# A selective-scan block with routing: two more of 32 slots get u from GpSimd, its statistics become powers and products, and x times D is made by ScalarE

## The chip, the cores and the metric

One core of one Trainium2 chip runs the whole kernel. The metric is device time in microseconds (us), the median over runs; the profile is of one further execution. The engines are named as in the profile: PE is TensorE, DVE VectorE, ACT ScalarE, POOL GpSimd, SP SyncE, which issues the transfers.

## The reference, cut to what matters

```python
x = resid + layernorm(mamba(layernorm(resid)))     # (2, 2048, 512)
out = x + layernorm(moe_bias(layernorm(x)))
# mamba: E = 1024 channels, N = 16 states
rn = r * rsqrt(mean(r * r) + eps) * norm_w
skip, x_in = rn @ W_skip, rn @ W_in
x = silu(conv4(x_in) + conv_b)
delta = softplus(x @ W_delta_1 @ W_delta_2 + b_delta_2)
B, C = x @ W_B, x @ W_C
h = h * exp(delta * A) + (delta * x) * B            # scan over time
y = sum_n(h * C) + x * W_D
mamba = r + (y * silu(skip)) @ W_out
# moe_bias: softmax over 64 experts, the 8 largest weights w
out = h2 * sum(w) + sum_k(w_k * expert_bias[k])
```

All is float32. A layernorm of rows needs their mean and variance, and x is normed twice in a row (layernorm, then the mean of squares).

## The kernel before, in words

The 2 x 2048 rows are cut into 16 chunks of T = 256. Six jobs work on a chunk one after another: norm, prep (projection, convolution, delta, B, C), scan, gate, mix (skip projection, y times silu(skip), W_out) and route (the second half of the reference). The loop is a pipeline of steps: in step i, chunk i + 3 is in norm, i + 2 in prep, i in scan, i - 1 in gate, i - 2 in mix and i - 3 in route. Each step has 32 slots. In each slot one scan unit is done: one of the 16 states for 256 of the channels over SPAN = 512 time steps, so a pair of chunks is scanned together. The order of work on each engine is written out by hand: every engine walks the same steps and slots, and side jobs stand at fixed slot numbers, `s`, counted from the job's own step (-4 is slot 28 of the step before, 41 is slot 9 of the step after).

A scan unit takes this way. ACT makes the decay exp(delta A) (`decay`, L728), and u = (delta x) B is made in one of two ways. In a **plain** slot POOL multiplies `dx_q` by `b_all`, a row of B that DMA has spread over all partitions, into `operand` (`make_u`, L597), and the decay goes to `bank` in PSUM. In a **turned** slot ACT scales the transposed `dx_t` by B (`make_ut`, L747, four instructions a slot), and PE transposes it back into `bank` (`turn_u`, L1152, eight a slot); the decay then goes to `operand`. `PLAIN_SLOTS` says which slots are plain. `bank` has no second buffer: whoever writes it, PE or ACT, waits for the scan before. `operand`, `h` and `hc` have three. DVE runs the scan itself (L971, two of 512 steps a slot), one slot's state over. POOL multiplies h by C (`weigh`, L613), one slot behind DVE, and PE transposes that onto `y_sum`, summing over the states (`add_y`, L1157), two slots behind. At the first of 16 states `add_y` also brings in x times D (L1175): a matmul of `x_q`, loaded from DRAM where `x` was stored, by `diag_d`, a diagonal matrix of D.

In its slot ACT first does the side jobs, then half of u two slots on, the first decay one slot on, the other half, the second decay. PE first transposes u for the next slot and adds y of two slots before, in turns, then does side work: the projections and transposes of the other jobs. DVE does its scan first, POOL first `weigh`, then `make_u` for two slots on.

Prep works on pairs of channel tiles, p = 0 to 3, at slots `TAPPED` = -5, 1, 6, 10: there ACT makes the convolution's first tap (`hv`, L709) and DVE the others (L1034); four slots on ACT makes the tanh (L816) and DVE `x` (L1017).

The statistics of four row blocks (xn, z, x1 and o; `mvx`, `mvz`, `mvh`, `mvo`) are started by DVE (`moments`, L946 and L949, mean and variance) and finished by POOL (`rstd` and `minus_mean_times`, L571 to L579), which adds eps, raises to the power -0.5 and multiplies by the negated mean, two values a partition. ACT then scales the rows with them (L709). After a small instruction whose result the next one needs, `link` makes the engine wait for it.

## Time and profile before

| | us |
|---|---|
| median of 3 runs | 2184.05 (2183.57 to 2187.59) |
| the profiled execution, its own time | 2178.91 |
| its span | 2177.1 |
| busy: PE matmul | 1893.4 (87%) |
| busy: POOL | 1859.3 (85%) |
| busy: DVE | 1726.6 (79%) |
| busy: ACT | 1716.2 (79%) |

The shares are over the whole span, which has a start of about 110 us before the first scan and an end of about 160 us after the last one, in which single chains of work run. The chain of work that ended last gives PE 31%, POOL 16%, DVE 15% and ACT 10% of the span.

### The profile page before, as it was taken

The page shows a single profiled execution, that of the slowest core. Times are in us where ns is not written, and L with a number is a line of the kernel's source. Part 1 is how long each engine was busy: PE and PEld are TensorE (multiplying, and loading weights), DVE is VectorE, ACT ScalarE, POOL GpSimd, SP SyncE. Part 2 cuts the span into 40 slices and gives each one's busy share as a digit, 9 for nine tenths or more (in the row PEclk, how much of TensorE's full clock was granted, in tenths as well). Part 3 has the DMA queues.
Part 4 walks back from the last instruction along what each step waited for, and adds up shares of the span by engine and source line. Part 5 has one row for each costly group of instructions (what it writes and reads, how often), then busy time and mean ns, then how long its engine had stood idle before and what let it go on. Part 6 is the DMA issues. An engine that isn't in the chain of part 4 may idle for free.

```text
span 2177.1 us, 35466 instructions
## 1 busy us (share of the span) xinstructions
PE 1893.4 (87%) x12005; PEld 1585.3 (73%) x12005; DVE 1726.6 (79%) x2529; ACT 1716.2 (79%) x3404; POOL 1859.3 (85%) x1256
## 2 busy tenths in 40 slices
PE   5677777999999998999999898999989898989883
PEld 4566767878787786878778786978778686767551
DVE  3487878898898989888888988888898978888332
ACT  3489797979888897979889897988889798888221
POOL 1299999899999999999999999999989899999312
PEclk9999898999999999999999999999999999999995
DMA  5656566765766575765756585765757464645310
GB/s 174 209 189 212 184 212 206 241 215 190 242 201 223 170 265 175 245 220 184 253 177 228 186 269 177 226 227 183 250 162 250 149 229 166 218 151 184 116 49 20
DMA packets 234672, 425.92 MB, mean 196 GB/s; under 512 B 18623, under 2 KB 134907, under 8 KB 234491
## 3 DMA queue, kind: packets, MB, share of 16 engines
q1 hardware_dynamic: 234490, 423.65, 59.0%
q8 instruction: 96, 1.57, 0.3%
q14 instruction: 86, 0.70, 0.1%
HBM read 339.18 MB, written 84.41 MB: 195 GB/s over the span
## 4 chain that ended last, share of the span: by engine, by line
PE 31%; POOL 16%; DVE 15%; ACT 10%; issue 7%; DMA 7%; DVEq 0%; SPq 0%; POOLq 0%; ACTq 0%
DVE h L971 10%; POOL hc L613 9%; PE mixed L1363 6%; PE bank L1152 6%; PE y_sum L1157 6%; PE pair_bank L1283 4%; DMA c_all<-bc_dram 4%; ACT u_t L747 3%; PE routed L1337 3%; POOL operand L597 2%; DVE hv L1034 2%; ACT operand L728 2%; DMA dx_q<-dx_dram 2%; PE routed L1237 1%; DMA dx_dram<-dx 1%
## 5 line engine op out<-in xcount | busy, mean ns | idle before, releaser
L613 POOL TENSOR_TENSOR hc<-h,c_all 128x1024 f32<-128x1024 f32 x512 | 1205.0, 2367 | 83.0 <-DVE h L971 76.0
L971 DVE TENSOR_TENSOR_SCAN h<-operand,carry,bank 128x512 f32<-128x512 f32 x528 | 649.2, 1266 | 126.1 <-PE bank L1152 112.7
L747 ACT ACTIVATE u_t<-dx_t,lbc 128x256 f32<-128x256 f32 x1408 | 631.8, 498 | 19.0 <-PE bank L1152 18.9
L1157 PE MATMUL y_sum<-ident,hc 128*128 128x128 f32 x4096 | 601.6, 278 | 7.5 <-POOL hc L613 6.8
L1152 PE MATMUL bank<-ident,u_t 128*128 128x128 f32 x2816 | 448.6, 284 | 165.5 <-DVE h L971 162.6
L1152 PEld LDWEIGHTS bank<-ident,u_t 128*128 128x128 f32 x2816 | 336.3, 145 | 274.1 <-issue 176.3
L1157 PEld LDWEIGHTS y_sum<-ident,hc 128*128 128x128 f32 x4096 | 490.7, 144 | 47.1 <-issue 27.5
L728 ACT ACTIVATE operand<-delta_q,neg_a 128x512 f32<-128x512 f32 x704 | 480.0, 711 | 0.0
L597 POOL TENSOR_TENSOR operand<-dx_q,b_all 128x1024 f32<-128x1024 f32 x160 | 378.4, 2365 | 8.4 <-DMA b_all<-bc_dram 8.4
L728 ACT ACTIVATE bank<-delta_q,neg_a 128x512 f32<-128x512 f32 x320 | 218.1, 682 | 204.1 <-DVE h L971 203.7
L971 DVE TENSOR_TENSOR_SCAN h<-bank,carry,operand 128x512 f32<-128x512 f32 x240 | 295.8, 1268 | 27.4 <-POOL operand L597 17.0
L1363 PE MATMUL mixed<-wout,ys 128*128 128x512 f32 x512 | 260.1, 602 | 3.5 <-DVE ys L1071 3.5
L1283 PE MATMUL pair_bank<-rnt,win 128*128 128x256 f32 x1024 | 247.5, 388 | 10.3 <-DVE x L1017 6.7
L1337 PE MATMUL routed<-rnt_gate,wskip 128*128 128x256 f32 x1024 | 245.3, 384 | 11.4 <-DVE thg L1059 11.4
L971 DVE TENSOR_TENSOR_SCAN h<-operand,bank 128x512 f32<-128x512 f32 x176 | 206.9, 1208 | 47.6 <-PE bank L1152 37.9
L1283 PEld LDWEIGHTS pair_bank<-rnt,win 128*128 128x128 f32 x1024 | 192.2, 195 | 46.2 <-issue 19.8
L1337 PEld LDWEIGHTS routed<-rnt_gate,wskip 128*128 128x128 f32 x1024 | 189.9, 193 | 36.9 <-issue 11.5
L1034 DVE SCALAR_TENSOR_TENSOR hv<-pair_bank,taps,hv 128x253 f32<-128x253 f32 (+2 forms) x384 | 184.3, 480 | 11.4
L1363 PEld LDWEIGHTS mixed<-wout,ys 128*128 128x128 f32 x512 | 81.2, 191 | 45.6 <-issue 40.9
L971 DVE TENSOR_TENSOR_SCAN h<-bank,operand 128x512 f32<-128x512 f32 x80 | 94.2, 1210 | 13.1 <-ACT bank L728 8.4
L1294 PE MATMUL pair_bank<-wlbc,x 128*128 128x160 f32 x512 | 85.7, 314 | 6.2 <-DVE x L1017 6.2
L667 POOL TENSOR_TENSOR dx<-delta,x 128x1024 f32<-128x1024 f32 x32 | 75.6, 2365 | 12.1 <-ACT delta L838 12.1
(119 smaller groups left out, 1858.5 us busy)
## 6 DMA issues: line engine op xcount, KB each, us to landing
c_all<-bc_dram SPq DMA_DIRECT2D x256, 512.0 KB, 4.3
b_all<-bc_dram SPq DMA_DIRECT2D x160, 256.0 KB, 5.5
win<-in_L_attn_W_in SPq DMA_DIRECT2D x64, 512.0 KB, 6.0
wskip<-in_L_attn_W_skip SPq DMA_DIRECT2D x64, 512.0 KB, 6.5
...
```

What stands on the lines that cost most here:

```text
L597: nc.gpsimd.tensor_tensor(operand[:, number % 3], dx_q[:, k], b_all[:, j % 2:j % 2 + 1].to_broadcast([P, 2, SPAN]), ALU.mult).then_inc(u_r ...
L613: nc.gpsimd.tensor_tensor(hc[:, number % 3], h[:, number % 3], c_all[:, j % 2, s % 2:s % 2 + 1].to_broadcast([P, 2, SPAN]), ALU.mult).then ...
L728: nc.scalar.activation(to, delta_q[:, k, q], ACT.Exp, scale=neg_a[:, et, n:n + 1]).then_inc(exp_ready.sem, 1)
L747: last = nc.scalar.activation(u_t[:, j % 2, b], dx_t[:, k, b], ACT.Copy, scale=lbc[:, stage % 2, b, DELTA + n:DELTA + n + 1])
L971: nc.vector.tensor_tensor_scan(h[:, number % 3, q], first, second, start, ALU.mult, ALU.add).then_inc(scan_done.sem, 1)
L1034: return nc.vector.scalar_tensor_tensor(out=to, in0=of, scalar=taps[:, et, k:k + 1], in1=onto, op0=ALU.mult, op1=ALU.add)
L1152: last = transpose(bank[:, q, b * P:(b + 1) * P], u_t[:, j % 2, b, q * P:(q + 1) * P], ident[:])
L1157: return matmul(to, lhsT=of, rhs=ident[:], is_transpose=True, start=start, stop=stop, skip_group_check=True)
L1283: last = matmul(pair_bank(p)[:, e * T:(e + 1) * T], win[:, p % 2, k, e * P:(e + 1) * P], rnt[:, k, :], start=(k == 0), stop=(k == KD - 1))
L1294: last = matmul(pair_banks[0][:, b * LBC:(b + 1) * LBC], x[:, et, b * P:(b + 1) * P], wlbc[:, et, :], start=(et == 0 and b == 0), stop=(et ...
L1337: last = matmul(routed[:, e * T:(e + 1) * T], wskip[:, p % 2, k, e * P:(e + 1) * P], rnt_gate[:, k, :], start=(k == 0), stop=(k == KD - 1))
L1363: last = matmul(mixed[:], ys[:, et, b * P:(b + 1) * P], wout[:, et, :], start=(et == 0), stop=(et == ET - 1))
```

## The change

It has four parts. Two more slots are plain, and the set is laid out anew: 6, 8 and 15 come in, 7 goes out. The product of x with D is made by ACT after `x` (new buffer `xd`, two of 128x256 for each pair, at slots `TAPPED` + 5 = 0, 6, 11, 15), stored in place of x, and PE brings it into `y_sum` by a transpose; `diag_d` is gone. DVE now delivers variance plus eps and the negated mean (two small reductions for each statistics, eps lies in a third column of `mv`), so that POOL is left with a power and a product; for xn both variances are raised to the power at once, four values. For o, whose rows are not divided by the softmax's sum, eps times that sum squared is made beforehand (slot 37), and half of DVE's reading of o is done a slot earlier. POOL's statistics of z move from slot 15 to 14, its addition of o from 45 to 47.

```diff
-PLAIN_SLOTS = (0, 2, 4, 7, 10, 13, 18, 22, 25, 29)
+PLAIN_SLOTS = (0, 2, 4, 6, 8, 10, 13, 15, 18, 22, 25, 29)
...
-                                        if v := due(sp, x_ready, t, p + 1):
-                                            sp.wait_ge(x_ready.sem, v)
+                                        if v := due(sp, xd_ready, t, p + 1):
+                                            sp.wait_ge(xd_ready.sem, v)
...
-                                        sp.dma_start(x_dram[side, :, 2 * p:2 * p + 2, part], x[:, 2 * p:2 * p + 2]).then_inc(
+                                        sp.dma_start(x_dram[side, :, 2 * p:2 * p + 2, part], xd[:, p % 2]).then_inc(
...
-                def rstd(to, at, var):
-
-                    link(nc.gpsimd.tensor_scalar(at, var, EPS, None, ALU.add))
-                    return nc.gpsimd.tensor_tensor(to, at, mhalf[:], ALU.pow)
-
-                def minus_mean_times(to, mv, r):
-                    link(nc.gpsimd.tensor_scalar(to, mv[:, :, 0], -1.0, None, ALU.mult))
-                    return times(to, to, r)
+                def rsqrt(to, of, halves):
+                    return nc.gpsimd.tensor_tensor(to, of, halves, ALU.pow)
...
-                                    link(rstd(now[:, 2], small["varx"][:], mvx[:, :, 1]))
-                                    link(times(small["ms"][:], mvx[:, :, 1], now[:, 2]))
-                                if s == -3:
-                                    link(times(small["ms"][:], small["ms"][:], now[:, 2]))
-                                    link(rstd(small["r2"][:], small["ms"][:], small["ms"][:]))
-                                if s == -1:
-                                    link(times(now[:, 0], now[:, 2], small["r2"][:]))
-                                    minus_mean_times(now[:, 3], mvx, now[:, 2])
-                                    minus_mean_times(now[:, 1], mvx, now[:, 0]).then_inc(s_ready.sem, 1)
...
+                                link(nc.gpsimd.tensor_scalar(small["varx"][:], mvx[:, :, 1], 1 + EPS, EPS * EPS, ALU.mult,
+                                                             ALU.add))
+                                link(rsqrt(now[:, 0:2], both_varx, mhalf[:]))
+                                times(now[:, 2:4], small["mx"][:].unsqueeze(1).to_broadcast([P, 2, TB]),
+                                      now[:, 0:2]).then_inc(s_ready.sem, 1)
...
-                                if s == 15:
+                                if s == 14:
...
-                                    link(rstd(small["rz"][:], small["varz"][:], mvz[:, :, 1]))
-                                    minus_mean_times(small["nz"][:], mvz, small["rz"][:]).then_inc(nz_ready.sem, 1)
+                                    link(rsqrt(small["rz"][:], small["varz"][:], mhalf[:, 0]))
+                                    times(small["nz"][:], small["nz"][:], small["rz"][:]).then_inc(nz_ready.sem, 1)
...
+                                if s == 37:
...
+                                    link(times(small["eo"][:], small["se"][:], small["se"][:]))
+                                    nc.gpsimd.tensor_scalar(mvo[:, :, 2], small["eo"][:], EPS, None,
+                                                            ALU.mult).then_inc(eo_ready.sem, 1)
...
-                                    link(times(var, mvo[:, :, 1], rs))
-                                    link(times(var, var, rs))
-                                    link(rstd(ro, var, var))
-                                    link(times(ro, ro, rs))
-                                    minus_mean_times(small["no"][:], mvo, ro).then_inc(no_ready.sem, 1)
-                                if s == 45:
+                                    link(rsqrt(small["ro"][:], small["varo"][:], mhalf[:, 0]))
+                                    times(small["no"][:], small["no"][:], small["ro"][:]).then_inc(no_ready.sem, 1)
+                                if s == 47:
...
+                                for p in range(PAIRS):
+                                    if s == TAPPED[p] + 5:
+                                        if v := due(act, x_ready, t, p + 1):
+                                            act.wait_ge(x_ready.sem, v)
+                                        if v := due(act, x_stored[p % 2], t, p // 2):
+                                            act.wait_ge(x_stored[p % 2].sem, v)
+                                        for et in (2 * p, 2 * p + 1):
+                                            last = nc.scalar.activation(xd[:, p % 2, et % 2], x[:, et], ACT.Copy,
+                                                                        scale=dskip[:, et:et + 1])
+                                        last.then_inc(xd_ready.sem, 1)
...
+                def and_eps(var, minus_mean, mv, ready):
+
                     for b in range(TB):
-                        last = nc.vector.bn_stats(stat6[:, b], of[:, b])
+                        last = nc.vector.bn_aggr(mv[:, b, 0:2], stat6[:, b])
                     link(last)
...
+                    nc.vector.tensor_reduce(minus_mean, mv[:, :, 0:1], axis=AX.X, op=ALU.add, negate=True)
+                    nc.vector.tensor_reduce(var, mv[:, :, 1:3], axis=AX.X, op=ALU.add).then_inc(ready.sem, 1)
...
-                                last = matmul(y_sum[:, b, q * P:(q + 1) * P], lhsT=x_q[:, q, b * P:(b + 1) * P],
-                                              rhs=diag_d[:, 2 * quarter + q], start=b % 2 == 0 and q == 0,
-                                              stop=False, skip_group_check=True)
+                                last = add_turned(y_sum[:, b, q * P:(q + 1) * P], x_q[:, q, b * P:(b + 1) * P],
+                                                  b % 2 == 0 and q == 0, False)
```

What this moves on POOL in the slots 2 to 10 of a steady step, from the u of slot 4 on; `operand<-dx_q,b_all` is a u, `hc<-h,c_all` a `weigh`. Before:

```order
L597 TENSOR_TENSOR operand<-dx_q,b_all 128x1024
L613 TENSOR_TENSOR hc<-h,c_all 128x1024 x3
L597 TENSOR_TENSOR operand<-dx_q,b_all 128x1024
L613 TENSOR_TENSOR hc<-h,c_all 128x1024 x3
L597 TENSOR_TENSOR operand<-dx_q,b_all 128x1024
L613 TENSOR_TENSOR hc<-h,c_all 128x1024 x2
```

And after the change:

```order
L593 TENSOR_TENSOR operand<-dx_q,b_all 128x1024
L609 TENSOR_TENSOR hc<-h,c_all 128x1024 x2
L593 TENSOR_TENSOR operand<-dx_q,b_all 128x1024
L609 TENSOR_TENSOR hc<-h,c_all 128x1024
L573 TENSOR_TENSOR stats<-stats 128x2
L687 TENSOR_SCALAR mvo<-stats 128x2
L609 TENSOR_TENSOR hc<-h,c_all 128x1024
L593 TENSOR_TENSOR operand<-dx_q,b_all 128x1024
L609 TENSOR_TENSOR hc<-h,c_all 128x1024 x2
L593 TENSOR_TENSOR operand<-dx_q,b_all 128x1024
L609 TENSOR_TENSOR hc<-h,c_all 128x1024 x2
L576 TENSOR_TENSOR stats<-stats,mhalf 128x2
```

The u of slot 7 has become those of 6 and 8, the two small rows between are the part of o's statistics that needs only the softmax's sum, and of the seven rows on o that stood behind the last pair of `hc` two are left, of which the first is shown.

A little further on in POOL's row, slots 11 to 16, from the u of slot 13 on. Before:

```order
L597 TENSOR_TENSOR operand<-dx_q,b_all 128x1024
L613 TENSOR_TENSOR hc<-h,c_all 128x1024 x2
L704 TENSOR_TENSOR o<-x1,o 128x1024
L613 TENSOR_TENSOR hc<-h,c_all 128x1024 x2
L575 TENSOR_SCALAR stats<-mvz 128x2
L576 TENSOR_TENSOR stats<-stats,mhalf 128x2
L579 TENSOR_SCALAR stats<-mvz 128x2
L571 TENSOR_TENSOR stats<-stats 128x2
L613 TENSOR_TENSOR hc<-h,c_all 128x1024
```

And after:

```order
L593 TENSOR_TENSOR operand<-dx_q,b_all 128x1024
L609 TENSOR_TENSOR hc<-h,c_all 128x1024 x2
L593 TENSOR_TENSOR operand<-dx_q,b_all 128x1024
L609 TENSOR_TENSOR hc<-h,c_all 128x1024
L576 TENSOR_TENSOR stats<-stats,mhalf 128x2
L573 TENSOR_TENSOR stats<-stats 128x2
L609 TENSOR_TENSOR hc<-h,c_all 128x1024
L699 TENSOR_TENSOR o<-x1,o 128x1024
L609 TENSOR_TENSOR hc<-h,c_all 128x1024
```

A u for slot 15 has come in, z's statistics stand a slot earlier with two rows in place of four, and the addition of o stands behind them.

On ACT, slots 4 to 7 of a steady step: `u_t<-dx_t` is half of a turned u, `bank<-delta_q` and `operand<-delta_q` are decays of a plain and of a turned slot. Before, from u of slot 6 on:

```order
L747 ACTIVATE u_t<-dx_t,lbc 128x256 x2
L728 ACTIVATE operand<-delta_q,neg_a 128x512
L747 ACTIVATE u_t<-dx_t,lbc 128x256 x2
L728 ACTIVATE operand<-delta_q,neg_a 128x512
L921 ACTIVATE low<-routed 64x256
L816 ACTIVATE pair_bank1<-hv 128x512
L728 ACTIVATE operand<-delta_q,neg_a 128x512 x2
L709 ACTIVATE xn<-xn,kept 128x512 x2
L709 ACTIVATE hv<-pair_bank0,cbias,taps 128x253 x2
L747 ACTIVATE u_t<-dx_t,lbc 128x256 x2
L728 ACTIVATE bank<-delta_q,neg_a 128x512
L747 ACTIVATE u_t<-dx_t,lbc 128x256 x2
```

And after:

```order
L723 ACTIVATE operand<-delta_q,neg_a 128x512 x2
L923 ACTIVATE low<-routed 64x256
L808 ACTIVATE pair_bank1<-hv 128x512
L742 ACTIVATE u_t<-dx_t,lbc 128x256 x2
L723 ACTIVATE bank<-delta_q,neg_a 128x512
L742 ACTIVATE u_t<-dx_t,lbc 128x256 x2
L723 ACTIVATE bank<-delta_q,neg_a 128x512
L704 ACTIVATE xn<-xn,kept 128x512 x2
L818 ACTIVATE xd<-x,dskip 128x256 x2
L704 ACTIVATE hv<-pair_bank0,cbias,taps 128x253 x2
L723 ACTIVATE operand<-delta_q,neg_a 128x512 x2
L742 ACTIVATE u_t<-dx_t,lbc 128x256 x2
```

The u of slots 6 and 8 is gone from here and that of slot 7 has come in; the decays of slot 6 go to `bank` and those of slot 7 to `operand`; the product with D stands between the scaling of xn and the first tap.

## Rows read from the trace of the kernel before

**Rows 1.** Stretches: us, busy us of PE, PEld, DVE, ACT, POOL (instructions), PEclk, DMA, GB/s

```profile
895.00:900.00 5.00, 5.00 (x32) 4.57 (x31) 4.74 (x9) 4.97 (x10) 5.00 (x4) 1.00 1.02 393
...
980.00:985.00 5.00, 3.37 (x28) 2.83 (x27) 4.96 (x10) 5.00 (x12) 4.39 (x9) 1.00 0.24 76
...
864.00:987.00 123.00, 113.76 (x750) 95.85 (x750) 108.90 (x160) 107.47 (x215) 116.78 (x79) 1.00 0.66 217
...
1848.00:1971.00 123.00, 108.82 (x715) 90.46 (x716) 104.39 (x131) 100.95 (x204) 121.08 (x69) 0.96 0.53 178
```

**Rows 2.** Waits from 500 to 1900 us: total us, times, longest us

```profile
ACT bank L728 <- DVE h L971: 148.0, 89, 5.2
...
DVE h L971 <- PE bank L1152: 109.5, 121, 2.7
...
POOL hc L613 <- DVE h L971: 55.7, 49, 2.3
```

**Rows 3.** Timeline of DVE, two scans: start us, us, what [idle before <- releaser]

```profile
964.83 2.45 DVE L971 TENSOR_TENSOR_SCAN h<-operand,carry,bank 128x512 f32<-128x512 f32 x2 [1.20 <-PE bank L1152]
...
977.58 2.45 DVE L971 TENSOR_TENSOR_SCAN h<-operand,carry,bank 128x512 f32<-128x512 f32 x2 [0.75 <-PE bank L1152]
```

**Rows 4.** Timeline of POOL, the statistics of z: start us, us, what

```profile
879.69 0.22 POOL L575 TENSOR_SCALAR stats<-mvz 128x2 f32<-128x2 f32 x1
...
1002.77 0.22 POOL L575 TENSOR_SCALAR stats<-mvz 128x2 f32<-128x2 f32 x1
1003.07 0.71 POOL L576 TENSOR_TENSOR stats<-stats,mhalf 128x2 f32<-128x2 f32 x1
1003.87 0.22 POOL L579 TENSOR_SCALAR stats<-mvz 128x2 f32<-128x2 f32 x1
1004.17 0.19 POOL L571 TENSOR_TENSOR stats<-stats 128x2 f32<-128x2 f32 x1
1004.32 2.36 POOL L613 TENSOR_TENSOR hc<-h,c_all 128x1024 f32<-128x1024 f32 x1
```

**Rows 5.** Groups of instructions: count | busy us, mean ns | idle before

```profile
L747 ACT ACTIVATE u_t<-dx_t,lbc 128x256 f32<-128x256 f32 x1408 | 631.8, 498 | 19.0 <-PE bank L1152 18.9
...
L1175 PE MATMUL y_sum<-diag_d,x_q 128*128 128x128 f32 x512 | 71.5, 285 | 0.0
...
L1017 DVE SCALAR_TENSOR_TENSOR x<-pair_bank,hv 128x512 f32<-128x512 f32 x64 | 43.4, 678 | 12.4 <-ACT pair_bank L816 12.4
...
L1115 DVE TENSOR_REDUCE stats<-top 128x2 f32<-128x16 f32 x16 | 2.5, 158 | 0.0
```

**Rows 6.** Timeline of PE weight loads: start us, us, what

```profile
892.96 0.97 PEld L1175 LDWEIGHTS y_sum<-diag_d,x_q 128*128 128x128 f32 x8
893.85 0.47 PEld L1157 LDWEIGHTS y_sum<-ident,hc 128*128 128x128 f32 x4
894.29 0.47 PEld L1353 LDWEIGHTS mixed<-ident,acc 128*128 128x128 f32 x4
```

**Rows 7.** Timeline of ACT before the first scan: start us, us, what

```profile
17.73 1.52 ACT L709 ACTIVATE xn<-xn,kept 128x512 f32<-128x512 f32 x2 [3.26 <-POOL kept L571]
...
34.27 0.60 ACT L816 ACTIVATE pair_bank<-hv 128x512 f32<-128x512 f32 x1 [3.59 <-DVE hv L1034]
...
34.80 1.00 ACT L709 ACTIVATE hv<-pair_bank,cbias,taps 128x253 f32<-128x253 f32 x2
```

**Rows 8.** Waits from 1750 to 2010 us: total us, times, longest us

```profile
DVE h L971 <- POOL operand L597: 14.7, 11, 2.4
```

**Rows 9.** The chain that ended last, final stretch: start us, us, what

```profile
2133.35 1.53 ACT o L709 x2
...
2134.95 2.34 POOL o L704
...
2139.71 0.81 ACT z L709
...
2165.29 1.30 DVE stat L946 x2
```

90 lines of the change are left out of this document (47 added, 43 removed).

## The prediction

> **What bounds the kernel now.** I read the busy shares by stretch first. A whole chunk in the steady part, 864 to 987 us, has no single full engine: GpSimd is busy 116.8 of 123 us, PE 113.8, VectorE 108.9, ScalarE 107.5 [rows 1]. One chunk takes 1002.77 - 879.69 = 123.1 us, from one statistics step of z to the next [rows 4]. Cut into 5 us pieces, the same chunk falls into two parts. In the first, call it A (slots 15 to about 3, some 75 us), PE and GpSimd show 5.00 of 5.00, ScalarE 4.97 and VectorE 4.74, in the piece from 895 [rows 1]. In the second, B (slots 4 to 14, some 45 us), VectorE is full at 4.96, PE has dropped to 3.37, in the piece from 980 [rows 1].
>
> Then the waits. From 500 to 1900 us, 11.4 chunks, VectorE's scans wait 109.5 us for PE's transposes of u, 9.6 us a chunk; ScalarE waits 148.0 us for scans before it may write the next decay into the single bank, 13.0 a chunk; GpSimd waits 55.7 us for scans, 4.9 a chunk [rows 2]. No wait of a scan for GpSimd's hc stands among the long ones. So GpSimd is nearly full but lags without holding anyone; in A the pace is set by PE's and ScalarE's queues, in B by VectorE, held up where PE's side work is ahead of the transposes: 1.20 us before the scan of slot 6, 0.75 us before that of slot 9 [rows 3]. GpSimd's 4.9 us are its only slack. Late in the program this changes: from 1848 to 1971 GpSimd is busy 121.08 of 123 us [rows 1], and scans wait 14.7 us for its u [rows 8]. There it is the bound.
>
> **The change part by part, per chunk.**
>
> GpSimd. Two more multiplies of 128x1024 at 2.36 us [rows 4]; back to back the next starts about 0.04 earlier: +4.64. The statistics of z go from four instructions to two. From start to start a scalar step takes 0.30, the power 0.80, the last product 0.15 [rows 4]: 1.55 becomes 0.95, -0.6; h the same, -0.6. Those of x have eleven instructions: four scalar steps (1.2), two powers (1.6), five products at 0.15 to 0.30 (about 1.3), together 4.1. Three remain, and their power has four values a row, which no row shows: 0.80 if the time is fixed, 1.60 if it goes by values. I take 1.2 (0.30 + 1.2 + 0.15 = 1.65), -2.4, with 0.4 either way. Those of o: seven instructions, 2.4, become 0.95 plus a product and a scalar step at slot 37 (0.45), -1.0. Sum: 4.64 - 4.6 = 0. In B the work grows by 4.64 + 0.95 (z moves in) - 1.4 (o) - 2.32 (the addition of o moves out to slot 15) = +1.9, inside the slack of 4.9; in A it falls by as much, which buys nothing there by itself.
>
> PE. Two slots' transposes go: four take 0.44 us from start to start [rows 6], eight 0.88, two slots 1.75. Slots 6, 8 and 15 turn plain, slot 7 turns back. The waits of rows 3 should both go: the scan of slot 6 needs no transpose, and before slot 9 PE no longer stands behind those of slot 8. That is 1.20 + 0.75 = 1.95. Slot 15's eight stood at the entry of A, 0.88 us; but ScalarE is full in A as well, so I credit 0.35. The product with D as a transpose: the eight matmuls of L1175 take 893.85 - 892.96 = 0.89, eight transposes 0.88 [rows 6]; nothing is gained. (The Trainium skill, "TensorE: Matmul & The Clock Gate", Terms, gives its transpose mode as four times faster for FP32. By that the 32 products with D would shrink from 3.6 to 0.9 us a chunk; the row says they already run at the transposes' pace.)
>
> ScalarE. Eight copies of u go, eight products x times D come, both 128x256, 0.498 each [rows 5]: 0. Each pair of the new ones is some 0.95 long and waits for x of that pair. They stand at slots 0, 6, 11 and 15; for slots 0, 6 and 11 the order has no u to make beside them, and ScalarE was waiting for scans thereabouts, which hides them. At slot 15 it goes into the time in which it waited for PE. Each new plain slot pins ScalarE to the scan before it, 148.0/89 = 1.66 us a time [rows 2]; in B that is free, since VectorE sets the pace. Queued behind are the copies of u two slots on and the decays of the next.
>
> VectorE. Each of four statistics gets two small reductions, 0.158 each [rows 5], nearer 0.3 with the link, against one reciprocal less. Those of x and h lie in A, under waits for PE; those of o and z in B, where VectorE is full: +0.6.
>
> Transfers. SP issues two more loads of b_all a chunk, each four slots ahead of the scan that needs its u and after the u two before it; the DMA engines are at 0.66 of a chunk [rows 1]: 0. The stores of x now wait for ScalarE's product, but SP is by then held by its loads of c_all, which follow GpSimd: 0. Were a load late, u would be, which is rival 3.
>
> Steady chunk: -1.95 - 0.35 + 0.6 = -1.7. Ten chunks have all six jobs: **-17**.
>
> First three chunks, no routing: GpSimd +4.64 - 2.4 = 2.2 each if it were full; it mostly isn't. I take +1 in all (0 to 6).
>
> Last chunks, no statistics of x to save: 4.64 - 0.6 - 0.6 - 1.0 = +2.4 each where GpSimd is the bound [rows 1, 8]; two of them, **+5**.
>
> Before the first scan. Nothing overlaps there. The tanh of a pair runs 34.27 to 34.87, and the next pair's first tap starts at 34.80 at once [rows 7]. Now x must come first (0.678 us [rows 5]), to 35.6, then its two products, to 36.5: +1.7, and the next pair +0.95, since ScalarE had xn to scale there. Two such chunks: 2 x 2.65 = +5.3. Against it the first xn waits 3.26 us for GpSimd's statistics [rows 7], which shrink by 2.4, less 0.35 for the reductions: -2. Sum **+3.5**. The removed diagonal matrices were made while ScalarE waited for those statistics: 0.
>
> After the last scan. Four statistics of o follow one another there, each with the chain behind it in ScalarE's queue: half of the reading is done a slot earlier (-0.65, half of the 1.30 of rows 9), reductions +0.3, GpSimd -1.4 (its part for the exponents' sum is off this chain): -1.7. The first two and the last give just that. At the third GpSimd makes z's statistics only after adding o (2134.95 to 2137.29), so ScalarE, done with o at 2134.88, starts the second half of z at 2139.71 and the first some 0.7 earlier, a gap of 4.1 us [rows 9]. Moved ahead, those statistics are ready when o is scaled: -1.7 - 4.0 = -5.7. h: -0.3. Together -1.7 - 1.7 - 5.7 - 0.3 - 1.7 = **-11**.
>
> Sum: -17 + 1 + 5 + 3.5 - 11 = -18.5. The profiled execution of before took 2178.9 us (span 2177.1), so the changed one would take 2160.4; the median of the three runs, 2184.05, lies 5.1 higher, and there I expect 2165.5. A change of less than 0.2%, 4.4 us, can hardly be told from none.
>
> **The rivals.**
>
> 1. Forecast, two waits in B and the tail: 2165. Chance 0.42.
>
> 2. More comes loose. PE and VectorE take turns in all of a chunk, and the 9.6 us of waits for PE's transposes [rows 2] shrink beyond the two that I named, until GpSimd's slack is gone: 123.1 - 4.9 = 118.2 a chunk. Half of that way, -3.5 a chunk instead of -1.7, gives another -18: about 2147; the whole way 2133. For it: they are 9.6 us a chunk, five times the 1.95 that I took. Against it: A's two full queues lose only 0.88 us. Chance 0.22.
>
> 3. GpSimd binds. Slots 6 and 8 each want u within a few slots in which three already lie; if GpSimd enters B several us behind, u is late for the scan and each scan waits. It decides where B's 4.9 us of slack are used up, and I put +1.9 into them. Price: the -1.7 is lost, the first and last three chunks pay 2.2 and 2.4 each (+13.8), the ends give 3.5 - 11: +6.3, 2190. Against it: GpSimd waits for scans right in B. Chance 0.14.
>
> 4. ScalarE binds, the case on the slower side that I fear most. At slot 14 it must now wait for both scans before A, where it is full and can't catch up. If it comes 1.66 us late [rows 2] into A, that is all paid: -1.35 + 1.66 = +0.3 a chunk, +4 over 13 chunks, +1 + 5 + 3.5 - 11: +2.5, 2187; with twice that wait 2208. For it: ScalarE is full in A [rows 1]. Against it: after slot 14 it had no wait to spare but for PE, and u for slot 15 (0.95 x 2) is gone there. Chance 0.11.
>
> 5. The sums cancel, within 4.4 us of before: 2184. Chance 0.08.
>
> 6. The transposes' pace is that of the page after all: A's PE queue holds the 32 products with D, 2.7 us shorter a chunk by three quarters of 3.6; if all of that comes out, 16 x 2.7 = 43 us more, 2123. (This is the rule of the page above.) The rows speak against it. Chance 0.03.
>
> **How the numbers follow.** The likeliest case with its unknowns (the power of four values, +-4 over ten chunks; the first chunks, 0 to 6; a third of the steady gain either way) runs from 2152 to 2179. To leave out no more than 2 in 10, the range reaches into rivals 2 and 4: 2142 to 2190. Faster by over 0.2%: nearly all of 1, all of 2 and 6, a fifth of 3 and 4, some of 5: 0.73. Same: 0.10. Slower: 0.17.
>
> **What the changed profile should show.** The chunk's period 121.4 us instead of 123.1. No wait of the scans of slots 6 and 9 for PE; GpSimd's waits for scans down from 4.9 to some 3 us a chunk; its u and hc unchanged at 2.36; the product with D at 0.11 us from start to start; ScalarE's waits for scans up by 1 to 3 us a chunk. Late chunks 2.4 us longer, with more than 14.7 us of scans waiting for u. Before the first scan the second pair's taps 1.7 us later. After the last, the end 11 us nearer to the last scan. Wrong would be: scans waiting for u in the steady part (rival 3), waits for ScalarE's decays or a long gap of PE at slots 14 to 20 (rival 4), or a period below 120 (rival 2).

## The result, and the profile after

The changed kernel takes 2162.78 us (median of 4 runs, 2160.2 to 2164.45) against 2184.55 for the kernel before on the same chip (2183.57 to 2187.59): a ratio of 0.9904, 95% interval 0.9892 to 0.9916. Its profiled execution took 2164.45 us, its span is 2162.3. The medians differ by 21.8 us, but the two profiled executions by 14.5 only: the one of before was faster than any of the runs that its median is taken from here (2178.91 us), the one of after was the slowest of its four. The parts in the table below add up to this smaller difference (14.7 by the spans), so some 7 us of the gain can't be put down to a part.

To see where the time went I cut each profiled execution at five marks of GpSimd's timeline: the start of the first `hc`, the starts of the additions to x1 (`x<-xp,z`) of chunks 0, 10 and 12, and the end of the last `hc`. All times are us.

| kernel | before the first hc | first chunks | ten steady chunks | two late chunks | to the last hc | after it |
|---|---|---|---|---|---|---|
| before | 115.8 | 402.8 | 1235.9 | 223.7 | 45.6 | 153.2 |
| after | 120.0 | 396.0 | 1228.3 | 229.4 | 44.7 | 143.9 |
| difference | +4.2 | -6.8 | -7.6 | +5.7 | -0.9 | -9.3 |

How far such parts scatter: the part before the first `hc` of five kernels with the same code there came to 116.8 to 121.8, the ten steady chunks of three kernels with the same code there to 1219.4, 1221.9 and 1224.9. A difference of 5 us between two single profiles proves nothing by itself.

Part of this scatter goes along with the clock that PE was granted. Those three kernels spent 37.5, 47.8 and 58.0 us of the stretch from 500 to 1740 us at the lower of its two levels (1.2 instead of 2.4 GHz, summed from the traces), in the same order as their times; after has 64.9 us there and the longest steady part of all that differ from it in side jobs alone (1228.3 against 1219.4 to 1224.9), before, with ten slots, 23.9. That is a correlation, and no run sets the clock by itself.

A steady chunk of after (columns as in [rows 1]):

```profile
850.00:973.00 123.00, 113.08 (x720) 94.40 (x718) 109.07 (x166) 106.77 (x213) 117.36 (x66) 0.97 0.68 219
```

Shares hardly move: a steady chunk looks as in [rows 1], with GpSimd 0.6 us fuller (and 1.1 us fuller, 122.16, in the late stretch from 1848 to 1971 us). The waits from 500 to 1900 us say more:

```profile
ACT bank L723 <- DVE h L981: 169.6, 103, 3.8
...
DVE h L981 <- PE bank L1167: 55.2, 56, 3.4
POOL hc L609 <- DVE h L981: 37.1, 56, 1.8
...
DVE h L981 <- ACT bank L723: 19.6, 14, 1.6
...
DVE h L981 <- POOL operand L593: 16.7, 12, 2.1
DVE h L981 <- ACT operand L723: 14.7, 25, 1.2
...
DVE h L981 <- POOL hc L609: 11.2, 9, 1.3
```

The scans' waits for PE have halved, 109.5 to 55.2 us [rows 2]. But waits for ScalarE and for GpSimd have come in their place: the last four rows sum to 62.2 us, where they were 25.9 before. Two thirds of what PE gave was taken back by the others.

The waits of [rows 3] are gone. The timeline of VectorE after, from the scan of slot 6 to that of slot 10:

```profile
957.36 2.45 DVE L981 TENSOR_TENSOR_SCAN h<-bank,carry,operand 128x512 f32<-128x512 f32 x2
...
970.45 2.44 DVE L981 TENSOR_TENSOR_SCAN h<-operand,carry,bank 128x512 f32<-128x512 f32 x2
...
974.40 0.15 DVE L954 TENSOR_REDUCE stats<-mvo 128x2 f32<-128x2 f32 x1
974.47 0.15 DVE L955 TENSOR_REDUCE stats<-mvo 128x2 f32<-128x4 f32 x1
974.53 2.45 DVE L981 TENSOR_TENSOR_SCAN h<-bank,carry,operand 128x512 f32<-128x512 f32 x2
```

No scan of slots 5 to 11 has a wait; the two new reductions take 0.13 us from start to start, not 0.3. I took the start of each slot's first scan over ten steady chunks: part B (from slot 4's to slot 15's) went from 43.04 to 41.27 us, part A (from slot 15's to the next slot 4's) from 80.51 to 81.45. So B gained 1.77 a chunk, and A lost 0.94. The wait before slot 15's scan lies in B by this cut.

The waits of the scans by slot, us a chunk, mean of the ten steady chunks 3 to 12, with the engine waited for, where length or engine changed by more than 0.3:

| slot | before | after |
|---|---|---|
| 6 | 1.28 PE | 0 |
| 9 | 0.71 PE | 0 |
| 15 | 0.86 PE | 0 |
| 16 | 1.05 PE | 0.70 ScalarE, 0.42 PE |
| 19 | 1.67 PE | 1.12 GpSimd's `hc`, 0.12 ScalarE |
| 21 | 0.93 PE | 0 |
| 22 | 0.48 ScalarE | 1.50 ScalarE |
| 25 | 0.14 ScalarE | 0.42 GpSimd's u, 0.14 ScalarE |
| 26 | 0.75 ScalarE | 0.39 ScalarE |
| 30 | 0.20 PE | 0.76 PE |

The first three are gained. Behind them what came makes up for what went (5.2 us before and 5.6 after in the other rows), and the added reductions come on top.

Two places in A show how it lost. The first is slots 21 and 22. Before (VectorE), the two scans waited 0.90 us for PE and 0.47 for ScalarE:

```profile
900.77 2.45 DVE L971 TENSOR_TENSOR_SCAN h<-operand,carry,bank 128x512 f32<-128x512 f32 x2 [0.90 <-PE bank L1152]
903.69 2.59 DVE L971 TENSOR_TENSOR_SCAN h<-bank,carry,operand 128x512 f32<-128x512 f32 x2 [0.47 <-ACT bank L728]
```

After (VectorE, then ScalarE), the first wait is gone and the second is 1.51, and it is 1.24 to 1.63 in each of the eleven chunks from 500 to 1760:

```profile
896.36 2.59 DVE L981 TENSOR_TENSOR_SCAN h<-bank,carry,operand 128x512 f32<-128x512 f32 x2 [1.51 <-ACT bank L723]
```

```profile
890.58 1.28 ACT L840 ACT_TABLE_LOAD   x1
891.88 1.57 ACT L840 ACTIVATE delta<-pair_bank,bdelta 128x256 f32<-128x256 f32 x4
...
894.24 1.28 ACT L723 ACT_TABLE_LOAD   x1
895.53 0.69 ACT L723 ACTIVATE bank<-delta_q,neg_a 128x512 f32<-128x512 f32 x1
```

The decay that the scan wants stands behind ScalarE's softplus of delta and two table loads of 1.28 us. A faster PE brings VectorE to that point earlier, and it waits there all the same: 1.41 us in slots 21 and 22 together before, 1.50 after.

The second is slot 30, in three of ten chunks. One of them, VectorE, then the weight loads of PE:

```profile
1052.91 2.45 DVE L981 TENSOR_TENSOR_SCAN h<-operand,carry,bank 128x512 f32<-128x512 f32 x2 [3.16 <-PE bank L1167]
```

```profile
1047.84 0.48 PEld L1218 LDWEIGHTS pair_bank<-ident,dx_q 128*128 128x128 f32 x4 [3.01 <-DMA dx_q<-dx_dram]
...
1051.75 0.14 PEld L1167 LDWEIGHTS bank<-ident,u_t 128*128 128x128 f32 x1 [0.33 <-issue]
```

PE waits 3.01 us for the load of the next quarter of `dx_q`, and its transposes of u stand behind that work. In the three chunks the scan of slot 30 waits 2.06 to 3.16 us; before it waited at most 0.64. PE waited for this load before as well, 1.72 us in the same chunk. Two things have come on top. The load landed 9.3 us after its issue instead of 8.1. And after its pause PE was granted only half the clock (columns as in [rows 1], PEclk third from the right):

```profile
1048.30:1051.60 3.30, 3.30 (x10) 1.97 (x9) 1.38 (x4) 1.69 (x4) 1.82 (x1) 0.51 1.04 394
```

From the first product behind the `dx_q` transposes to the first transpose of u it took 3.44 us (1048.31 to 1051.75), where before took 1.84 for the same instructions at full clock: 1.6 of the 3.16 us. Of the other two chunks one shows the half clock too, one doesn't.

GpSimd's small work, its timeline after: z's two rows, and xn's three:

```profile
868.93 0.70 POOL L576 TENSOR_TENSOR stats<-stats,mhalf 128x2 f32<-128x2 f32 x1
869.71 0.19 POOL L573 TENSOR_TENSOR stats<-stats 128x2 f32<-128x2 f32 x1
...
926.51 0.19 POOL L626 TENSOR_SCALAR stats<-mvx 128x2 f32<-128x2 f32 x1
926.79 1.01 POOL L576 TENSOR_TENSOR kept<-stats,mhalf 128x4 f32<-128x4 f32 x1
927.88 0.20 POOL L573 TENSOR_TENSOR kept<-stats,kept 128x4 f32<-128x4 f32 x1
```

From start to start z's take 0.78 and 0.19 at least, and xn's 0.28 + 1.09 + 0.15 = 1.52, where I had 1.65. The late waits (1750 to 2010 us) rose from 14.7 us [rows 8]:

```profile
DVE h L981 <- POOL operand L593: 22.7, 14, 2.8
```

The products with D have become fewer on PE, and this the prediction overlooked. In the source they are 16 a chunk and 256 in all, before as after. The trace of before counts 512 of them [rows 5], so each of these FP32 matmuls stands there as two instructions; after the change the count is

```profile
L1172 PE MATMUL y_sum<-ident,x_q 128*128 128x128 f32 x256 | 39.9, 280 | 0.0
```

and the weight loads of one group of four products, of after, set against the 0.97 us x8 of [rows 6]:

```profile
883.02 0.47 PEld L1172 LDWEIGHTS y_sum<-ident,x_q 128*128 128x128 f32 x4
883.46 0.47 PEld L1172 LDWEIGHTS y_sum<-ident,hc 128*128 128x128 f32 x4
```

Four products took 0.89 us from start to start as matmuls by the diagonal and take 0.44 as transposes: 3.6 and 1.8 us a chunk. PE is relieved of 1.8 us a chunk by them, besides the 1.75 of the two slots.

### The profile page after: what moved, and what is told of

It is laid out like the page before. It is cut to its first block and busy times, and to the rows that moved or that the text cites. A ratio compares the mean times of both kernels' runs of the same rounds, so it can differ in the third digit from the quotient of the medians.

```text
span 2162.3 us, 34280 instructions
## 1 busy us (share of the span) xinstructions
PE 1858.5 (86%) x11493; PEld 1537.7 (71%) x11493; DVE 1739.2 (80%) x2641; ACT 1710.8 (79%) x3396; POOL 1878.4 (87%) x1051
## 3 DMA queue, kind: packets, MB, share of 16 engines
q8 instruction: 92, 1.51, 0.3%
## 5 line engine op out<-in xcount | busy, mean ns | idle before, releaser
L981 DVE TENSOR_TENSOR_SCAN h<-operand,carry,bank 128x512 f32<-128x512 f32 x480 | 591.0, 1268 | 87.2 <-PE bank L1167 60.8
L742 ACT ACTIVATE u_t<-dx_t,lbc 128x256 f32<-128x256 f32 x1280 | 574.4, 498 | 0.3 <-PE bank L1167 0.3
L1167 PE MATMUL bank<-ident,u_t 128*128 128x128 f32 x2560 | 412.9, 286 | 183.8 <-DVE h L981 181.9
L1167 PEld LDWEIGHTS bank<-ident,u_t 128*128 128x128 f32 x2560 | 306.6, 146 | 286.4 <-issue 205.6
L593 POOL TENSOR_TENSOR operand<-dx_q,b_all 128x1024 f32<-128x1024 f32 x192 | 454.8, 2369 | 15.0 <-DMA b_all<-bc_dram 14.1
L723 ACT ACTIVATE bank<-delta_q,neg_a 128x512 f32<-128x512 f32 x384 | 262.0, 682 | 233.4 <-DVE h L981 232.8
L723 ACT ACTIVATE operand<-delta_q,neg_a 128x512 f32<-128x512 f32 x640 | 433.4, 712 | 0.0
L981 DVE TENSOR_TENSOR_SCAN h<-bank,carry,operand 128x512 f32<-128x512 f32 x288 | 354.6, 1268 | 48.2 <-POOL operand L593 26.5
L981 DVE TENSOR_TENSOR_SCAN h<-operand,bank 128x512 f32<-128x512 f32 x160 | 188.3, 1209 | 35.2 <-PE bank L1167 24.0
L981 DVE TENSOR_TENSOR_SCAN h<-bank,operand 128x512 f32<-128x512 f32 x96 | 112.9, 1211 | 17.6 <-ACT bank L723 11.5
L1375 PEld LDWEIGHTS mixed<-wout,ys 128*128 128x128 f32 x512 | 82.0, 193 | 45.6 <-issue 40.9
L659 POOL TENSOR_TENSOR dx<-delta,x 128x1024 f32<-128x1024 f32 x32 | 75.6, 2364 | 12.3 <-ACT delta L840 12.3
```

The costliest lines, as they stand in the source:

```text
L593: nc.gpsimd.tensor_tensor(operand[:, number % 3], dx_q[:, k], b_all[:, j % 2:j % 2 + 1].to_broadcast([P, 2, SPAN]), ALU.mult).then_inc(u_r ...
L723: nc.scalar.activation(to, delta_q[:, k, q], ACT.Exp, scale=neg_a[:, et, n:n + 1]).then_inc(exp_ready.sem, 1)
L742: last = nc.scalar.activation(u_t[:, j % 2, b], dx_t[:, k, b], ACT.Copy, scale=lbc[:, stage % 2, b, DELTA + n:DELTA + n + 1])
L981: nc.vector.tensor_tensor_scan(h[:, number % 3, q], first, second, start, ALU.mult, ALU.add).then_inc(scan_done.sem, 1)
L1167: last = transpose(bank[:, q, b * P:(b + 1) * P], u_t[:, j % 2, b, q * P:(q + 1) * P], ident[:])
L1375: last = matmul(mixed[:], ys[:, et, b * P:(b + 1) * P], wout[:, et, :], start=(et == 0), stop=(et == ET - 1))
```

## The experiments

Twelve kernels, each with the ratio to before and its 95% interval; their profiled executions cut at the same marks:

| run | median us | ratio | before first hc | first | steady | late | after last hc |
|---|---|---|---|---|---|---|---|
| old slots | 2163.08 | 0.9898 (0.9877 to 0.9918) | 121.8 | 398.2 | 1236.3 | 222.5 | 143.9 |
| slots only | 2194.68 | 1.0047 (1.0032 to 1.0063) | 115.6 | 402.2 | 1242.3 | 234.1 | 154.6 |
| taps first | 2149.99 | 0.9840 (0.9823 to 0.9856) | 114.5 | 393.7 | 1221.9 | 229.4 | 143.9 |
| light o, after | 2141.50 | 0.9804 (0.9781 to 0.9827) | 117.5 | 395.9 | 1212.1 | 226.6 | 139.2 |
| light o, before | 2176.29 | 0.9963 (0.9950 to 0.9976) | 115.9 | 403.6 | 1235.7 | 220.1 | 151.3 |
| moves back | 2159.44 | 0.9888 (0.9873 to 0.9903) | 118.5 | 395.2 | 1224.0 | 228.8 | 146.0 |
| fewer late | 2138.98 | 0.9803 (0.9786 to 0.9819) | 113.4 | 393.4 | 1224.9 | 219.2 | 140.5 |
| few late | 2136.12 | 0.9782 (0.9766 to 0.9798) | 114.9 | 394.1 | 1219.4 | 219.1 | 143.8 |
| taps first, old slots | 2157.68 | 0.9880 (0.9865 to 0.9895) | 112.7 | 396.9 | 1234.0 | 223.0 | 143.9 |
| quarter of x times D | 2159.05 | 0.9887 (0.9866 to 0.9907) | 116.8 | 394.6 | 1222.4 | 229.7 | 143.9 |
| fewer late, moves back | 2139.18 | 0.9800 (0.9783 to 0.9816) | 114.0 | 393.7 | 1219.5 | 220.2 | 142.2 |
| few late, moves back | 2138.46 | 0.9787 (0.9766 to 0.9809) | 115.2 | 395.1 | 1220.7 | 217.0 | 142.2 |

**Old slots: the change without its slots.**

```diff
-PLAIN_SLOTS = (0, 2, 4, 6, 8, 10, 13, 15, 18, 22, 25, 29)
+PLAIN_SLOTS = (0, 2, 4, 7, 10, 13, 18, 22, 25, 29)
```

> The changed kernel with the ten plain slots of before; statistics, product with D and moved steps stay. Theory 1 (the two more u pay in the steady chunks and cost in the last ones, where GpSimd is the bound): the ten steady chunks lose some 1.3 us each against the changed kernel, the last two win back 2 x 2.8, the first three lose a part of their 6.8: 2163 + 13 - 6 + 4 = about 2174. Theory 2 (the lighter statistics alone make the gain, the slots add nothing): 2163 or less, about 2155.

As a whole the two extra plain slots give nothing: 2163.08 against 2162.78. By parts they give 8.0 us in the steady chunks, 2.2 in the first and take 6.9 in the late ones. Against before this kernel gains 9.3 us after the last `hc` and 4.6 in the first chunks; the steady chunks with lighter statistics, PE's lighter products with D and ten slots (1236.3) are those of before (1235.9). ScalarE is fuller in this run: from 500 to 1740 us it is busy 1103.2 us, 1071.4 before and 1075.6 in the changed kernel, since it makes the products with D on top of all the copies of u. So the two slots relieve PE and ScalarE at once, and no run parts the two.

**Slots only: before with the twelve.** The same edit on the kernel before, the other way round.

> The kernel before with only the set of twelve plain slots. Theory 1 (GpSimd's slack of 4.9 us a chunk is used up by the 4.64 of two u, and its lateness then holds the scans): steady chunks within 1 us of before, the last three 4.6 us each longer, the first ones about as before: 2184 + 12 = 2196, up to 2210. Theory 2 (GpSimd only lags and holds nobody, PE's relief is what counts): faster than before, about 2175.

Slower, by 0.5%. The waits from 500 to 1740 us:

```profile
DVE h L971 <- PE bank L1152: 70.9, 72, 6.3
DVE h L971 <- POOL operand L597: 35.8, 26, 3.2
```

The scans now wait 35.8 us for GpSimd's u, where before had no such wait in this stretch, and GpSimd's own waits for scans are down from 54.7 to 7.7. The rest of the change, that is the lighter statistics together with the products with D and the moves, is thus worth 14.0 us in the steady chunks with twelve slots (1242.3 to 1228.3) and nothing with ten. The parts don't add. That it is the lighter statistics that make room for the slots is argued from the 35.8 us of waits for u, which are 4.2 in the changed kernel; no run has the twelve slots and the products without them.

**Taps first.** ScalarE's products of x and D stand behind the taps of the next pair (the whole block also moves below the taps' code).

```diff
-                                    if s == TAPPED[p] + 5:
+                                    if s == TAPPED[p] + (5 if p else 6):
```

> The changed kernel, ScalarE's product with D put behind the next pair's first tap (the first pair's a slot later, the others in the same slot). Theory 1 (before the first scan the product stands in the way of the taps, 2.65 us in each of two chunks): first u and the whole kernel 4 to 5 us earlier, 2158. Theory 2 (VectorE or PE hides it, or the product in slot 1 comes in the way of decays in each of the 16 chunks): no change or up to 5 us slower, 2163 to 2168.

13 us shorter than the change as given, and the intervals don't meet. ScalarE before the first scan, taps first:

```profile
32.54 0.60 ACT L808 ACTIVATE pair_bank<-hv 128x512 f32<-128x512 f32 x1 [3.59 <-DVE hv L1043]
33.07 1.00 ACT L704 ACTIVATE hv<-pair_bank,cbias,taps 128x253 f32<-128x253 f32 x2
33.97 0.90 ACT L840 ACTIVATE xd<-x,dskip 128x256 f32<-128x256 f32 x2
```

and in the changed kernel:

```profile
16.34 1.52 ACT L704 ACTIVATE xn<-xn,kept 128x512 f32<-128x512 f32 x2 [4.20 <-POOL kept L573]
...
33.09 0.60 ACT L808 ACTIVATE pair_bank<-hv 128x512 f32<-128x512 f32 x1 [3.59 <-DVE hv L1043]
34.45 0.91 ACT L818 ACTIVATE xd<-x,dskip 128x256 f32<-128x256 f32 x2 [0.76 <-DVE x L1026]
35.26 0.99 ACT L704 ACTIVATE hv<-pair_bank,cbias,taps 128x253 f32<-128x253 f32 x2
```

From the tanh's start to the next tap's it is 0.53 us with the taps first (32.54 to 33.07) and 2.17 in the changed kernel (33.09 to 35.26): the products cost the path 1.64 there. The gain of the part before the first `hc` is 5.5 between these two profiles, 4.8 between the means of the five kernels with the products ahead and the six with them behind. The first chunks give 2.3 and the steady ones 6.4 more. There the product stood in ScalarE's row ahead of the next pair's first tap, for which VectorE's taps wait; the waits from 500 to 1740 us, of after and of taps first:

```profile
DVE hv L1043 <- ACT hv L704: 11.7, 18, 1.1
```

```profile
DVE hv L1043 <- ACT hv L704: 8.9, 10, 1.1
```

In part B this wait falls from 0.35 to 0.03 us a chunk, and 0.57 of the 0.62 us by which the period of the scans shrinks lie in B; in the first chunks (118 to 500 us) it falls from 3.8 to 1.5 us. The wait at slot 22 stays at 1.50, so the product has no part in that one. These waits show 3.2 of the steady 6.4 us; the rest is within the scatter, and the clock was granted more freely in this run (47.8 us at the lower level, 64.9 in the changed kernel).

**Light o, on after and on before.** The addition of x1 and o on 8 of 512 columns (the signal behind it is cut here).

```diff
-nc.gpsimd.tensor_tensor(o[:], x1[:], o[:], ALU.add)
+nc.gpsimd.tensor_tensor(o[:, :, 0:8], x1[:, :, 0:8], o[:, :, 0:8], ALU.add)
```

> The changed kernel with GpSimd's addition x1 + o made on 8 of 512 columns, so that most of out lacks x1: 2.1 us of GpSimd less in each chunk with routing, nothing else changed. Theory 1 (GpSimd is now a co-bound in the steady chunks): 1 to 2 us less a chunk, with 2 x 2.1 in the last two and 2 us at the end some 15 to 25 us less: 2140 to 2148. Theory 2 (GpSimd holds nobody in the steady chunks, other waits took up what PE set free): only the last chunks and the end, 6 us: 2157.

> The kernel before, with GpSimd's addition of x1 and o done on 8 of its 512 columns, so that o's other columns are wrong: that part of the output is left out, and GpSimd has some 2.1 us less to do in each chunk. The same cut on the changed kernel took 16.2 us off its ten steady chunks (1228.3 to 1212.1 us) and 21 us in all. Theory A (the change turned GpSimd from an engine that lags into one that sets the period): here the ten steady chunks stay within 4 us of 1235.9, the chunks after them give some 2 us and the end 4.7 us, in all about 2177 us. Theory B (GpSimd set the period before as well): the steady chunks lose 12 to 18 us here too, in all about 2162 us.

This is the clearest pair. 2.1 us of GpSimd's work a chunk are worth 1.6 a chunk after the change and 0.0 before it (1235.9 and 1235.7). So GpSimd only lagged before and has a share in the pace after. The 1.6 is at the upper end: the profiled execution of light o on after is the fastest of its four. Its slowest (2146.82 us) had the same mean granted clock as the changed kernel, 0.955, and lies 13 to 18 us under the changed kernel's four runs; less the 7.5 us of the late chunks and the end, 0.6 to 1.0 a chunk are left. The waits from 500 to 1740 us, of the light kernel before, and then of the light kernel after:

```profile
DVE h L971 <- PE bank L1152: 93.9, 108, 1.8
...
POOL hc L613 <- DVE h L971: 76.3, 62, 2.3
```

```profile
POOL hc L609 <- DVE h L981: 46.5, 86, 1.4
...
PEld pair_bank L1218 <- DMA dx_q<-dx_dram: 2.6, 3, 1.3
...
DVE h L981 <- POOL hc L609: 1.5, 1, 1.5
```

On before, what was cut turned into GpSimd's own waits for scans (54.7 us in the same stretch of before, 76.3 now). On after, the scans' waits for GpSimd's `hc` went from 11.2 to 1.5 us, but they all lay at slot 19, and there the scan now waits as long for ScalarE (the scans' waits for its decays of turned slots rose from 14.2 to 31.2 us): nothing is gained by that. What is gained lies at slots 25, 30 and 31, 0.42, 0.76 and 0.36 us a chunk. PE's waits for `dx_q` fell from 11.0 to 2.6, and the waits at slot 30 don't occur in the ten chunks. In chunk 7 of the light kernel the scan of slot 30 starts 31.2 us behind that of slot 22, as before (31.5), where the changed kernel has 34.5. GpSimd makes dx (L659), which goes out and comes back as `dx_q`; here it is 1.2 us earlier, and so is the issue of the load (18.6 us behind the scan of slot 22, not 20.0). That is a way by which GpSimd's lateness reaches VectorE, through PE. It isn't lateness against before, where the load was issued at 20.0 as well: what is new is the longer landing and PE's half clock, and an earlier dx avoids both.

**Moves back.** The statistics of z and the addition of o at their slots of before (and o's store, from slot 48 to 47, cut here).

```diff
-                                if s == 14:
+                                if s == 15:
...
-                                if s == 47:
+                                if s == 45:
```

> The changed kernel with its three moves undone: the statistics of z at slot 15, the addition of x1 and o at slot 45 and its store at slot 47, as before. Theory A (the moves matter only after the last scan, where z's row norm then ran ahead of o's addition): the last part grows from 143.9 us by the 3 to 4 us that the prediction gave it, the rest stays, about 2166 us. Theory B (they carry nothing, since what is done at a slot number depends only on the order around it): within 1.5 us of 2162.8. Theory C (the addition two slots earlier holds back hc at slot 46 and 47): steady chunks 0.5 us longer each, about 2168 us.

At the end the moves are worth 2.1 us (143.9 to 146.0), half of what I gave them; nothing in the run shows that they help before it. By medians the two can't be told apart.

**Quarter of x times D.** One of the four transposes for each pair of row blocks, the whole loop replaced.

```diff
-for b in (2 * pair, 2 * pair + 1):
-    for q in range(2):
-        last = add_turned(y_sum[:, b, q * P:(q + 1) * P], x_q[:, q, b * P:(b + 1) * P], b % 2 == 0 and q == 0, False)
+last = add_turned(y_sum[:, 2 * pair, 0:P], x_q[:, 0, 2 * pair * P:(2 * pair + 1) * P], True, False)
```

> The changed kernel with one of four of PE's transposes that bring x times D into y: three quarters of that term of y are left out, and PE has 24 fewer of them in each chunk, 2.7 us at 0.11 each. This is the price that the sixth rival put on those products. Theory A (PE's queue sets the pace in the longer part of a chunk): most of it comes out, 16 x 2.7 = 43 us at the most, 2120 to 2135 us, with 23 us or more out of the ten steady chunks' 1228.3. Theory B (GpSimd, which after the change loses 16 us where 21 are taken from it, sets the pace, and PE's waits only come round to it): under 8 us out of the steady chunks, 2150 to 2160 us. Both at once: about half, 2140 us.

The expectation has the size wrong by a factor of two, for the reason given above: the changed kernel has 16 such transposes a chunk and this one 4 (256 and 64 in the traces), so 12 go, 1.3 us a chunk. They are worth 0.6 a chunk, within the scatter (2159.05 against 2162.78, with intervals that overlap). Of its waits, 500 to 1740 us:

```profile
PE bank L1167 <- DVE h L981: 100.1, 81, 2.9
```

What was cut, 13 us in ten chunks, turned up again as PE's own wait for scans (87.3 to 100.1 in that stretch). So PE by itself doesn't set the pace of the changed kernel; a share of up to the 0.6 us isn't excluded.

**Taps first with old slots.** As old slots, on taps first.

> The changed kernel with the products of x and D behind the taps and with the ten plain slots of before in all chunks; it is set against the same kernel with twelve (2149.99 us; ten steady chunks 1221.9 us in its profiled run) and against the run with old slots and the products ahead of the taps (2163.08; 1236.3). Theory A (the two more slots relieve PE, and that is worth the 8 us they gave in the steady chunks of the changed kernel, whatever ScalarE's order): steady chunks about 1230, late chunks 7 us shorter than with twelve, in all about 2151 us. Theory B (with ten slots PE's transposes set the pace so much that ScalarE's order is hidden): steady chunks stay at 1236, about 2156 us. Theory C (the slots gave nothing but room for ScalarE's products): steady chunks about 1222, about 2143 us.

Between theories A and B: 1234.0, so the slots are worth 12.1 us in the steady chunks once the products are out of ScalarE's way, against 8.0 with them in it, and 7.7 in all (2157.68 to 2149.99). Theory C is out. The order of ScalarE gives 2.3 in the steady chunks with ten slots and 6.4 with twelve. With ten, VectorE's taps wait for ScalarE nowhere in part B, in either order, so there is nothing to gain there; the scans' waits for PE are still 66.8 us. The differences between 8.0 and 12.1 and between 2.3 and 6.4 are smaller than the scatter of single profiles.

**Fewer and few late.** The set of slots becomes a function of the chunk; the counts on the semaphores follow it.

```diff
...
+MANY = (0, 2, 4, 6, 8, 10, 13, 15, 18, 22, 25, 29)
+FEWER = (0, 2, 4, 7, 10, 13, 18, 22, 25, 29)
+FEW = (0, 4, 8, 13, 17, 21, 25, 29)
+def plain_slots(t):
+    return MANY if FIRST + t < 13 else FEWER if FIRST + t < 14 else FEW
...
```

(In the run with fewer late, `FEWER` in all of chunks 13 to 15.)

> The changed kernel with the products of x and D behind the taps, and with the ten slots of before in the last three chunks (13 to 15) alone; it is set against the same kernel with twelve throughout (2149.99 us, of that 229.4 us between the additions of chunks 10 and 12, where the kernel before took 223.7 us). Theory A (in the last chunks GpSimd is bound, and the two more u cost it what they take): these 229.4 us go back to 223 or 224, about 2143 us. Theory B (the longer stretch comes from elsewhere): it stays at 229, 2150 us.

> As the run with fewer late, with ten slots in chunk 13 and eight (0, 4, 8, 13, 17, 21, 25, 29) in chunks 14 and 15. If GpSimd still binds there with ten, two fewer give 4.7 us in each of two chunks, less what PE's four more products add: about 2138 us. If TensorE or VectorE take over there, 2143 to 2148 us, with waits of VectorE for PE's bank in the last two chunks.

With fewer late, the late chunks lose 10.2 us, more than the 5.7 that the change had put on them, and the median 11.0. GpSimd is still full there, but the others have drawn nearer. The stretch from 1760 to 1980 us, of after and of fewer late:

```profile
1760.00:1980.00 220.00, 183.72 (x1160) 145.17 (x1159) 178.38 (x232) 171.45 (x338) 216.24 (x107) 0.96 0.57 188
```

```profile
1760.00:1980.00 220.00, 189.24 (x1245) 151.97 (x1246) 189.55 (x243) 184.70 (x371) 217.38 (x108) 0.98 0.58 196
```

Eight slots in two chunks give no more (219.1 against 219.2; the medians' intervals overlap): by then the scans wait for PE, 25.9 us between 1740 and 1990, 21.4 with ten. Why ten slots in chunks 13 to 15 alone leave 219.2 and ten slots throughout 223.0 isn't settled; the mark itself lies on GpSimd, which may come to it further behind the scans with twelve slots. Nor was the shorter end of that run (140.5) followed.

**Both with the moves back while scans run.**

```diff
-                                if s == 14:
+                                if s == (15 if FIRST + t < 16 else 14):
...
-                                if s == 47:
+                                if s == (45 if FIRST + t < 15 else 47):
```

> The kernel with the products behind the taps and ten slots in chunks 13 to 15 (2138.98 us), and besides, as long as scans run, the statistics of z at slot 15 and the addition of x1 and o at slot 45 as before; after the last scan they stay at 14 and 47. The moves undone gave 4.3 us in the steady chunks (1228.3 to 1224.0) and cost 2.1 at the end. Theory A (both are real): about 2135 us. Theory B (the 4.3 us are the scatter of single profiled runs, which differed by 5.5 us over the same code in three kernels): 2139 us.

> The same with eight plain slots in chunks 14 and 15 (2136.12 us without the moves undone). Theory A: about 2132 us. Theory B: 2136 us.

Theory B: 2139.18 and 2138.46 against 2138.98 and 2136.12, no difference that the intervals would show. The best of all is few late, 2136.12 us, 0.9782 of before and 1.2% under the changed kernel; the four of this group can't be told apart.

## Why the prediction was right, point by point

**The time and its direction** came out (forecast 2165.5, measured 2162.8), and that owes something to luck: of the sum's terms the steady chunks gave 9.4 us less than put, the first chunks 7.8 us more, and the two cancelled. Between the profiled executions the terms add to -14.7, where -18.5 was forecast and the medians show -21.8; some 7 us of the measured gain belong to no term.

**Two waits in B: right.** Both waits of [rows 3] are gone, 1.99 us a chunk on the mean where 1.95 had been put. VectorE's four pairs of reductions cost less than 0.3 each; but those of x and h, put at nothing under waits for PE, add to A (0.4 us, less the reciprocal) as those of o and z do to B (0.6).

**Entry of A, -0.35: wrong**, and with it the silence about the rest of A. The wait at slot 15 went altogether, 0.86 us. But behind it A lost 0.94. I had argued that A would at worst stay. PE's relief there was passed on: at slots 21 and 22 ScalarE's softplus gives back what PE gives, at slots 19, 25 and 30 GpSimd, ScalarE and the `dx_q` load do (light o, up to 16.2 us in ten chunks). **ScalarE's products hidden at slots 0, 6 and 11: wrong** in part; they held up VectorE's taps in B (taps first, 3.2 us of waits in ten chunks, up to 6.4 in time). Steady -7.6 instead of -17.

**Product with D on PE, put at nothing: wrong.** I read the eight instructions of L1175 in [rows 6] as eight products. They are four, and as transposes they take half the time. PE was relieved of 3.5 us a chunk, twice what I had put; that the steady chunks gained less than half of the forecast all the same makes the miss in A the larger.

**GpSimd's net of 0, inside its slack: the sum was right, the conclusion wrong.** From 500 to 1900 us its waits for scans fell from 55.7 to 37.1 us, 3.3 a chunk where some 3 were forecast. All its waits from 500 to 1740 us are 46.7 us after and 56.7 before, 4.6 and 5.7 a chunk; period (122.8 and 123.6) less waits is 118.2 and 117.9: its work hardly changed. But the slack lay in B (4.4 of its 5.0 us of waits for scans a chunk in the ten steady ones; 2.0 of 3.4 after the change), and in A it was short. Rival 3 was too simple as well: scans wait for u only 4.2 us in the 1240 of the steady part, and the period didn't rise. Its mechanism came in part, by another road, `dx_q` and PE.

**First three chunks, +1: wrong, -6.8.** I priced GpSimd alone and left out PE's products with D, 1.8 us a chunk. The scans wait for PE there too, from 118 to 500 us, of before and then of after:

```profile
DVE h L971 <- PE bank L1152: 29.5, 34, 2.5
POOL hc L613 <- DVE h L971: 18.0, 23, 2.7
```

```profile
DVE h L981 <- PE bank L1167: 21.3, 19, 2.7
...
POOL hc L609 <- DVE h L981: 6.8, 8, 1.5
```

The scans' waits for PE shrank by 8.2 us, and GpSimd paid out of its own waits, 18.0 to 6.8. The slots aren't what did it in the main: with ten slots (old slots) the part is already 4.6 us shorter, and these waits are 22.5. What of the 4.6 comes from the products and what from the statistics isn't parted.

**Last chunks, +5: right** at +5.7, with 22.7 us of waits for u. Taken back by fewer late.

**Before the first scan, +3.5: right** at +4.2, and +3.2 between the means of the five and of the three kernels with the same code there. The products cost 1.64 where 1.7 was put, and taps first, which keeps the gain at xn, comes out 1.3 under before; xn starts at 16.34 instead of 17.73, 1.39 earlier and not 2.

**After the last scan, -11: mechanism right, one size off**, -9.3. The chain that ended last, after:

```profile
2122.21 1.30 DVE stat L947 x2
...
2125.08 2.31 POOL o L699
2127.55 2.35 POOL x L674
...
2151.70 1.29 DVE stat L947 x2
```

From the reading of z to that of x1 it is now 2129.92 - 2122.21 = 7.71 us, in the run with moves back 9.83, before 12.01. The moves give 2.1, not the 4.0 of the gap: z's halves are ready early, but the addition of o now stands ahead of that of x1 on GpSimd and ends 0.17 us before it. The last statistics of o gave 1.2 instead of 1.7, since its two halves are read together there.

**Rival 6** (the transposes' pace is that of the page) had something in it. The Trainium skill ("TensorE: Matmul & The Clock Gate", Terms) gives its transpose mode as four times faster for FP32; here it came to twice, 3.6 to 1.8 us a chunk. Its second half, that all of this comes out of the time, fails: where a further 13 us were taken from PE in ten chunks, at most 5.9 came out (quarter of x times D). **Rival 2** (more comes loose) began: the scans' waits for PE fell from 94.3 us to 42.0 between 500 and 1740, 5.2 a chunk and not 2.3 (2.3 of them already with ten slots, 71.4 us), but ScalarE and GpSimd took most of them up. **Rival 4** (ScalarE binds) has a part in that, at slot 22 and not at slot 14, where I had looked: ScalarE's waits for scans rose from 148.0 to 169.6, 1.9 a chunk as forecast, and scans' waits for its decays from 16.2 to 31.5 us between 500 and 1740.
